# Attention and expert layer on one core: terms of Q and K interleaved by rows, one stacking DMA for both heads, the front work of batches 0 to 2 in another order

## Chip, cores and metric

One core of one Trainium2 chip runs the kernel. The metric is the device time of one execution, in microseconds (us), lower is better: the median of several runs.

## What is computed

The layer takes x [8, 256, 256] (8 batches of 256 tokens, 256 features) and a context of the same shape. It returns x + attention, and on top of that x + a mixture of experts:

```
q, k, v = LN(x) @ Wq.T, ctx @ Wk.T, ctx @ Wv.T      (16 heads of 16 features)
p       = softmax(where(masks, q @ k.T / 4, -inf))
x       = x + (p @ v) @ Wo.T + bo
gate    = softmax(LN(x) @ w_gate.T);  the best 2 of 8 experts for each token
x       = x + sum over the 2: score * (gelu(LN(x) @ W1[e] + b1[e]) @ W2[e] + b2[e])
```

Everything is float32. The masks are inputs (all true here).

## The kernel before, in words

**Two stages.** The attention stage works through 8 batches, in 64 steps of two heads (MP = 8 steps a batch). The expert stage then multiplies lists of 256 tokens with the weights of one expert at a time. Each engine has its own program over the same step numbers s = -16 to 84 (START, LAST), and semaphores tie them together. What is done at which step stands in tables: FRONT (lines 95 and 96) gives, for each batch n, the step 8n + offset of each piece of front work, and BACK, ROUTE and the LATE tables give what comes later. `due[s]` (lines 115 to 123) is what every engine reads, and the order of the work inside one step is the order of the `if` lines of that engine.

**Front work of a batch.** `load` (SP, lines 272 to 280) fetches x, ctxT and the mask of the batch. DVE takes the statistics of LN (`statistics`, line 454), POOL the inverse deviation (line 377) and the normalised rows (line 383; for batch 0 DVE does it, line 472). PE projects K from ctxT (`project`, line 747), turns the normalised rows (`turn_rows`, line 739), projects Q, and later V (`token_product`, line 755). These products are plain float32.

**Terms and stacking.** The scores need float32 precision from a faster type (fp32r), so a number is held as hi + lo. ACT writes hi (`split_high`, line 644), DVE the rest lo (`split_low`, line 447), both 128 partitions x 512 numbers in `flat`. `stack` (SP, lines 282 to 296) then copies them into K[n % 4] and Q[n % 4]. In these tiles head pair m of a batch is a slice of 256 numbers, the first head of the pair lives in partitions 0 to 63, the second in 64 to 127 (r = 0, 1; HALF = 64). Each half holds three terms of 16 rows, one after the other (TERMS = 3, D = 16): hi, hi, lo for K and hi, lo, hi for Q, so that one matmul over 48 rows gives three partial products. For each of the 3 terms and each half there is one DMA: 6 for K and 6 for Q, each of 128 KB, from 128 source partitions into 16 neighbouring ones:

```
for r in range(2):
    a = r * HALF + c * D
    done.after(sp.dma_start(dst[a:a + D]..., src[:, r, :]...))
```

**Two passes of scores.** In step s, `scores_for_max` (line 771) multiplies Q by K over the 48 rows into S1, and DVE takes the negated row maxima (`take_max`, line 479). LAG = 10 steps later `scores` (line 793) multiplies K by Q over 50 rows into S2: rows 48 and 49 of each half hold ones in K and the maxima as hi and lo in Q, so that the maxima are subtracted by the matmul. The maxima of a batch are turned by PE (`turn_maxima`), written to mT by ACT and put into Q by two DMAs that ACT issues (`maxima_out`, line 654). The ones are put into the four K tiles once, by 8 DMAs (`ones_rows`, line 298, at step -5). ACT then takes the exponential of S2 (line 678) and `weighted` (line 815) multiplies by V. S1 and S2 are one buffer each: S1 of step s waits for the maximum of step s - 1, S2 for the exponential before it.

**The masks' branch.** DVE reduces all masks to one flag (`least_mask`, line 432, called behind the first `q_split`), PE checks it by a matmul at step FLAG = -1 (`open_keys`, line 735), DVE writes any_mask (line 441), and PE reads it into a register and takes the branch without masks (lines 922 to 926). All steps s >= 0 of PE lie inside that branch.

**Small loads.** ACT issues all eight loads of weights and small inputs before anything else (`act_loads`, line 260). Many consumers wait for all small ones together (LOADS_SMALL).

**Where the zero rows come from.** `pool_constants` (line 340) makes ident, the zero tile and other constants on POOL. DVE starts its loop once all of them are there.

## Time and profile before

| what | us |
|---|---|
| median of 3 runs (583.44 to 587.05) | 586.22 |
| the profiled execution itself | 579.65 |
| its span, first to last instruction | 578.4 |

The profile comes from one execution. Its span is what the rows below add up to, and its own time is 1.25 us longer. PE is TensorE's matmuls, PEld its weight loads, DVE VectorE, ACT ScalarE, POOL GpSimd, SP the engine that issues most DMAs (SPq and ACTq are the queues' issue instructions). The attention stage fills the span up to about 266 us, the experts the rest. L789 is line 789 of the kernel. A mean of granted clock of 1.00 is 2.4 GHz, 0.50 is 1.2 GHz.

### The profile page before, as it was taken

To read this page: it belongs to the slowest core of one execution; us is meant where nothing else is said; L and a number is where in the kernel's file an instruction comes from. 1 tells how busy PE (TensorE), PEld (TensorE's weight loads), DVE (VectorE), ACT (ScalarE), POOL (GpSimd) and SP (SyncE) were. 2 spreads that over 40 slices of the span, in tenths; PEclk is the share of its full clock that TensorE was granted. 3 is DMA by queue.
4 is the path that set the end of the run, shared out by engine and by line. 5 is a ranking of instruction groups with operands and counts; after the bars stand their busy time and mean duration, and the time that the engine had idled before them with its cause. 6 is when DMAs were issued, how large, how long until landed. Compare 5 with 4: busy or idle time off the path is not lost.

```text
span 578.4 us, 10606 instructions
## 1 busy us (share of the span) xinstructions
PE 482.1 (83%) x3874; PEld 418.6 (72%) x3874; DVE 376.1 (65%) x736; ACT 344.8 (60%) x567; POOL 175.9 (30%) x191
## 2 busy tenths in 40 slices
PE   5546989999989858272299999699999999999994
PEld 4334656666756536151299999699999999999994
DVE  3455566866776744125568878568888788878871
ACT  1112566666566343211488788478887888778870
POOL 4320330352322654503302234204222432234324
PEclk9779799999999876656599999989999999999998
DMA  7976786867640911201555678969886878768713
GB/s 195 152 123 108 125 151 126 132 142 165 118 75 14 341 64 67 93 0 57 163 198 179 206 229 248 219 230 266 242 253 197 248 227 259 225 213 248 216 20 37
DMA packets 77637, 94.99 MB, mean 164 GB/s; under 512 B 7808, under 2 KB 70528, under 8 KB 77568
## 3 DMA queue, kind: packets, MB, share of 16 engines
q1 hardware_dynamic: 67344, 82.44, 52.4%
q0 software_dynamic: 8160, 10.38, 9.4%
q10 hardware_dynamic: 2080, 1.49, 0.9%
q8 instruction: 32, 0.52, 0.4%
q14 instruction: 21, 0.17, 0.1%
HBM read 63.96 MB, written 17.34 MB: 141 GB/s over the span
## 4 chain that ended last, share of the span: by engine, by line
PE 67%; issue 9%; DMA 7%; DVE 5%; ACT 4%; POOL 3%; SPq 2%; ACTq 1%; another core or an unknown queue 0%; POOLq 0%; DVEq 0%
PE h_bank L1079 21%; PE y_bank L1092 20%; PE bank L751 6%; PE bank L759 5%; PE bank L823 4%; PE S L789 3%; PE S L811 2%; PE bank L743 2%; PE x_bank L1063 2%; DMA cin<-in_ctxT 2%; DVE nmax L485 2%; POOL lists L404 2%; DMA xin<-in_x 2%; PE bank L831 1%; DMA xg<-lists 1%
## 5 line engine op out<-in xcount | busy, mean ns | idle before, releaser
L1186 POOL DMA_INDIRECT out<-y,slot x46 | 83.6, 1817 | 212.2 <-DVE y L1307 202.4
L1079 PE MATMUL h_bank<-xgT,W1p 128*128 128x256 f32 x1104 | 144.1, 288 | 1.8 <-DVE xgT L1278 1.8
L1079 PEld LDWEIGHTS h_bank<-xgT,W1p 128*128 128x128 f32 x1104 | 138.0, 194 | 2.2 <-issue 2.2
L1092 PE MATMUL y_bank<-W2p,hp 128*128 128x256 f32 x1104 | 136.0, 282 | 0.0
L1092 PEld LDWEIGHTS y_bank<-W2p,hp 128*128 128x128 f32 x1104 | 133.9, 188 | 0.0
L485 DVE TENSOR_REDUCE nmax<-S 128x4 f32<-128x1024 f32 x64 | 78.3, 1224 | 55.9 <-PE S L789 50.9
L683 ACT ACTIVATE prob<-S 128x1024 f32<-128x1024 f32 x64 | 65.8, 1028 | 43.2 <-PE S L811 26.7
L1293 DVE TENSOR_TENSOR hp<-hf,hp 128x512 fp32r<-128x512 f32 x92 | 63.6, 691 | 35.4 <-ACT hp L1152 35.3
L1253 DVE TENSOR_TENSOR W1p<-w_in,W1p 128x1024 fp32r<-128x1024 f32 x46 | 56.2, 1226 | 21.1 <-ACT W1p L1117 21.0
L1144 ACT ACTIVATE hf<-h_bank,b1c 128x256 f32<-128x256 f32 x120 | 49.7, 466 | 27.5 <-PE h_bank L1079 27.5
L1260 DVE TENSOR_TENSOR W2p<-w_in,W2p 128x1024 fp32r<-128x1024 f32 x46 | 56.3, 1225 | 10.1 <-ACT W2p L1126 10.1
L1152 ACT ACTIVATE hp<-hf 128x512 fp32r<-128x512 f32 x92 | 58.3, 634 | 2.9
L381 POOL TENSOR_TENSOR rstd<-ve,half 128x2 f32<-128x2 f32 x16 | 11.4, 714 | 155.7 <-DVE ve L470 155.6
L1117 ACT ACTIVATE W1p<-w_in 128x1024 fp32r<-128x1024 f32 x46 | 47.9, 1046 | 13.8 <-DMA w_in<-in_W 9.0
L1126 ACT ACTIVATE W2p<-w_in 128x1024 fp32r<-128x1024 f32 x46 | 48.0, 1046 | 0.0
L789 PE MATMUL S<-K,Q 48*128 48x256 f32 x256 | 33.4, 340 | 15.3 <-DVE nmax L485 13.1
L789 PEld LDWEIGHTS S<-K,Q 48*128 48x128 f32 x256 | 19.9, 192 | 34.0 <-DVE nmax L485 18.8
L404 POOL DMA_INDIRECT lists<-x2n,rows x32 | 32.7, 1022 | 26.5 <-DVE rows L587 18.1
L823 PE MATMUL bank<-prob,V 128*32 128x256 f32 x512 | 37.2, 412 | 1.2 <-ACT prob L683 1.2
L1144 ACT ACTIVATE hf<-h_bank,b1T 128x256 f32<-128x256 f32 x64 | 26.5, 466 | 16.5 <-PE h_bank L1079 16.5
L811 PE MATMUL S<-Q,K 50*128 50x256 f32 x256 | 29.5, 310 | 5.8 <-ACT prob L683 5.0
L751 PE MATMUL bank<-cin,WkT 128*128 128x256 f32 x64 | 22.6, 513 | 11.4 <-DMA cin<-in_ctxT 11.4
(140 smaller groups left out, 519.3 us busy)
## 6 DMA issues: line engine op xcount, KB each, us to landing
w_in<-in_W SPq DMA_DIRECT2D x46, 1024.0 KB, 8.9
K<-flat_k SPq DMA_DIRECT2D x48, 128.0 KB, 4.3
Q<-flat_q SPq DMA_DIRECT2D x48, 128.0 KB, 4.3
xg<-lists SPq DMA_DIRECT2D x23, 265.0 KB, 5.5
lists<-zero SPq DMA_DIRECT2D x17, 265.0 KB, 4.8
b_in<-in_b SPq DMA_DIRECT2D x23, 128.0 KB, 6.6
xin<-in_x SPq DMA_DIRECT2D x8, 256.0 KB, 4.9
cin<-in_ctxT SPq DMA_DIRECT2D x8, 256.0 KB, 5.3
```

The costliest lines, as they stand in the source:

```text
L485: max_done.after(dve.tensor_reduce(nmax[n % 4][:, :, :, m].rearrange("p t r -> p r t"), S1[:].rearrange("p r (t k) -> p r t k", t=TT), AX. ...
L683: exp_done.after(act.activation(prob[s % 4][:].rearrange("p r t l -> p (r t l)"), S2[:].rearrange("p r l -> p (r l)"), ACT.Exp, scale=SCALE))
L751: i = pe.matmul(b[:, m * L:(m + 1) * L], w[:, kc, m * P:(m + 1) * P], src[:, kc, :], start=(kc == 0), stop=(kc == KC - 1))
L789: i = pe.matmul(S1[:, r, t * L:(t + 1) * L], Q[n % HELD][a, m, t * P:(t + 1) * P], K[n % HELD][a, m, :], start=not masked, stop=(not maske ...
L823: i = pe.matmul(b[j * OS:(j + 1) * OS, 0:L], V[n % 3][:, t, r * MP + m, :], prob[(MP * n + m) % 4][:, r, t, :], start=(t == 0), stop=(t == ...
L1079: ins = pe.matmul(h_bank[pair][:, u, :], W1p[k][a][:, kc, m * P:(m + 1) * P], xgT[k][c][:, kc, :], start=(j == 0), stop=(j == len(terms) - 1))
L1092: ins = pe.matmul(y_bank[k][:, t, :], hp[k][a][:, m, t * P:(t + 1) * P], W2p[k][c][:, m, :], start=(j == 0), stop=(j == len(terms) - 1))
L1144: h_act.after(act.activation(hf[pair % 2][:, u], h_bank[pair][:, u], ACT.Gelu, bias=bias[:, m:m + 1]))
L1152: h_hi.after(act.activation(hp[i % 2][0][:, c], hf[pair % 2][:], ACT.Copy))
L1186: st_y[i % 4].after(pool.indirect_dma_start(out=out, out_offset=bass.IndirectOffsetOnAxis(ap=slot[i % 4][:, t:t + 1], axis=0), in_=y[i % 2 ...
L1260: w2_lo.after(dve.tensor_tensor(W2p[i % 2][1][:, c], w2_in[i % 2][:, c], W2p[i % 2][0][:, c].bitcast(F32), ALU.subtract))
L1293: h_lo.after(dve.tensor_tensor(hp[i % 2][1][:, c], hf[pair % 2][:], hp[i % 2][0][:, c].bitcast(F32), ALU.subtract))
```

## The change

**Layout.** The three terms of a row now lie in neighbouring partitions: term c of row d is partition 4d + c of a half (ROWS = 4), and the fourth partition of each group of four is spare. A half is 64 rows of 16 x 4. Both heads of a pair are written by the same DMA: 32 partitions, every fourth of 128, from the 128 source partitions. The weights' columns are reordered on the host to fit. The spare rows hold zeros in Q (but the four that receive the maxima, which one DMA of ACT writes) and in K zeros and two rows of ones in each half (`corner`); `spare_rows` fills them with two DMAs of 32 partitions x 8 KB a tile, at steps -12, 1, 3 and 5. For batches 4 to 7 one more small DMA clears the four rows of the maxima before Q is stacked. Both passes of scores now read all 64 rows.

**Order.** FIRST_FRONT gives batches 0, 1 and 2 steps of their own. PE does nothing for batch 1 before the branch; FLAG is -4. ACT's loads are spread over steps. ctxT is loaded ahead of x, and the masks ahead of the batch's own mask. Batch 1 is normalised by DVE. `unread` puts matmuls over 512 columns of bf16, whose result nothing reads, into PE's program: 12 at step -6, 12 at step 0, 3 at each of the steps 1 to 9.

```diff
     HELD = 4
+    ROWS = TERMS + 1
+    FIRST_MAX = ROWS * (D - 2) + TERMS
...
                  q=-7, q_split=-6, q_stack=-6, mask_q=-3, v=-1, v_out=0, mrep=7, mx=8)
+    FIRST_FRONT = {
+        0: dict(load=-16, ln1=-13, norm1=-11, residual=5, k=-11, k_split=-10, k_stack=-10, xn=-8, xT=-7, q=-7, q_split=-6,
+                q_stack=-6, mask_q=-3, v=4, v_out=5, mrep=7, mx=8),
+        1: dict(load=-5, ln1=0, norm1=1, residual=6, k=1, k_split=2, k_stack=2, xn=2, xT=3, q=3, q_split=4, q_stack=4,
+                mask_q=5, v=6, v_out=7, mrep=15, mx=16),
+        2: dict(load=5, ln1=7, norm1=8, residual=9, k=8, k_split=9, k_stack=9, xn=10, xT=11, q=11, q_split=12, q_stack=12,
+                mask_q=13, v=15, v_out=16, mrep=23, mx=24)}
...
         for name, o in FRONT.items():
-            due[MP * n + o][name] = n
+            due[FIRST_FRONT[n][name] if n in FIRST_FRONT else MP * n + o][name] = n
...
-        ones = sb(first, "ones", [2, MP * L])
+        line = sb(first, "line", [2 * D, L])
...
+        blank = zero[0:2 * D, 0:1, 0:L].to_broadcast([2 * D, MP, L])
+        corner = line[:].rearrange("p (o l) -> p o l", o=1).to_broadcast([2 * D, MP, L])
...
-        k_ones = signal("k_ones", 16)
+        k_ones = [signal(f"k_ones{i}", 16) for i in range(HELD)]
...
+        def act_loads(s):
+            if s == START:
+                ld_wk.after(act.dma_start(WkT[:], WkT_in.rearrange("(k p) f -> p k f", p=P)))
+                ld_wq.after(act.dma_start(WqT[:], WqT_in.rearrange("(k p) f -> p k f", p=P)))
+                ld_pad.after(act.dma_start(pad_c[:], pad_c_in))
+            if s == -4:
+                ld_wv.after(act.dma_start(WvT[:], WvT_in.rearrange("(k p) f -> p k f", p=P)))
+            if s == 1:
+                ld_bo.after(act.dma_start(bo_b[:], bo.rearrange("(o e) -> o e", o=1).to_broadcast([P, E])))
+            if s == 6:
+                ld_wo.after(act.dma_start(WoT[:], WoT_in.rearrange("(k p) f -> p k f", p=P)))
+            if s == 7:
+                ld_small.after(act.dma_start(WgT[:], wgT_in.rearrange("(k p) e -> p k e", p=P)))
+                ld_small.after(act.dma_start(b1T[:], b1T_in))
...
                     sp.wait_ge(mask_q.sem, TT * (n - 1))
+                ld_c[n % 2].after(sp.dma_start(cin[n % 2][:], c_d[n]))
                 ld_x[n % 2].after(sp.dma_start(xin[n % 2][:], x_d[n]))
-                ld_c[n % 2].after(sp.dma_start(cin[n % 2][:], c_d[n]))
+                if n == 0:
+                    ld_masks.after(sp.dma_start(masks_in[:], mask.rearrange("n q k -> (n q k)")
...
                 if n >= HELD:
                     sp.wait_ge(s2_done.sem, MP * (n - HELD + 1))
+                    if which == "q":
+                        done.after(sp.dma_start(over_heads(dst[FIRST_MAX:FIRST_MAX + 4 * ROWS:ROWS]), blank[0:4]))
                 sp.wait_ge(sem, end - 1)
                 for c, src in order:
                     if src is lo:
                         sp.wait_ge(sem, end)
-                    for r in range(2):
-                        a = r * HALF + c * D
-                        done.after(sp.dma_start(dst[a:a + D].rearrange("p m l -> p (m l)").bitcast(F32),
-                                                src[:, r, :].bitcast(F32)))
-
-            def ones_rows():
-                sp.wait_ge(dve_const.sem, 1)
-                for i in range(HELD):
-                    for r in range(2):
-                        a = r * HALF + TERMS * D
-                        k_ones.after(sp.dma_start(K[i][a:a + 2].rearrange("p m l -> p (m l)").bitcast(F32), ones[:]))
+                    done.after(sp.dma_start(dst[c:P:ROWS].rearrange("p m l -> p (m l)").bitcast(F32),
+                                            src[:].rearrange("p k l -> p (k l)").bitcast(F32)))
+
+            def over_heads(rows_):
+                return rows_.bitcast(F32)
+
+            def spare_rows(i):
+                if i == 0:
+                    sp.wait_ge(pool_rows.sem, 4)
+                q_stacked[i].after(sp.dma_start(over_heads(Q[i][TERMS:P:ROWS]), blank[:]))
+                k_ones[i].after(sp.dma_start(over_heads(K[i][TERMS:P:ROWS]), corner[:]))
 
...
                     load(now["load"])
-                    if now["load"] == 0:
-                        ld_masks.after(sp.dma_start(masks_in[:], mask.rearrange("n q k -> (n q k)")
-                                                    .rearrange("(p f) -> p f", p=P)))
                 if "k_stack" in now:
                     stack("k", now["k_stack"])
                 if "q_stack" in now:
                     stack("q", now["q_stack"])
-                if s == -5:
-                    ones_rows()
+                if s == -12:
+                    spare_rows(0)
+                if s in (1, 3, 5):
+                    spare_rows(s // 2 + 1)
...
         def pool_constants():
+            pool_rows.after(pool.memset(zero[:, :, 0:E], 0.0))
+            pool_rows.after(pool.memset(line[:], 1.0))
+            pool.wait_ge(pool_rows.sem, 2)
+            pool_rows.after(pool.affine_select(out=line[:], in_=line[:], compare_op=ALU.is_ge, fill=0.0,
+                                               base=2 - D, pattern=[[0, L]], channel_multiplier=1))
+            pool.wait_ge(pool_rows.sem, 3)
+            pool_rows.after(pool.affine_select(out=line[:], in_=line[:], compare_op=ALU.is_ge, fill=0.0,
+                                               base=D + 1, pattern=[[0, L]], channel_multiplier=-1))
...
-            pool_const.after(pool.memset(zero[:, :, 0:E], 0.0))
...
-                    if now["norm1"]:
+                    if now["norm1"] > 1:
...
                 if s == FLAG:
                     all_open()
+                if s == 1:
+                    dve.wait_ge(pe_misc.sem, filled_by("xn", 0))
+                    normalise(0, 1)
                 if "k_split" in now:
                     split_low("k", now["k_split"])
+                    if now["k_split"] == 0:
+                        least_mask()
                 if "q_split" in now:
                     split_low("q", now["q_split"])
-                    if now["q_split"] == 0:
-                        least_mask()
...
                 if n:
-                    act.wait_ge(*stacked(q_stacked if which == "q" else k_stacked, n - 1, 2 * TERMS))
+                    act.wait_ge(*(stacked(q_stacked, n - 1, ROWS) if which == "q" else stacked(k_stacked, n - 1, TERMS)))
...
             def maxima_out(n):
                 if n:
-                    act.wait_ge(*stacked(m_stacked, n - 1, 2))
+                    act.wait_ge(*stacked(m_stacked, n - 1, 1))
                 evacuate("mx", n, mT[:], lambda ps: ps[0:4 * MP, 0:L])
                 act.wait_ge(*emptied_at("mx", n))
                 if n >= HELD:
                     act.wait_ge(s2_done.sem, MP * (n - HELD + 1))
-                for r in range(2):
-                    a = r * HALF + TERMS * D
-                    m_stacked[n % HELD].after(act.dma_start(
-                        Q[n % HELD][a:a + 2].rearrange("p m l -> p (m l)").bitcast(F32),
-                        mT[2 * MP * r:2 * MP * (r + 1), :]))
+                m_stacked[n % HELD].after(act.dma_start(
+                    Q[n % HELD][FIRST_MAX:FIRST_MAX + 4 * ROWS:ROWS].rearrange("p m l -> p (m l)").bitcast(F32), mT[:]))
 
             def query_mask(n):
...
                 now = due[s]
+                act_loads(s)
...
                 if m == 0:
-                    pe.wait_ge(*stacked(k_stacked, n, 2 * TERMS))
-                    pe.wait_ge(*stacked(q_stacked, n, 2 * TERMS))
+                    pe.wait_ge(*stacked(k_stacked, n, TERMS))
+                    pe.wait_ge(*stacked(q_stacked, n, ROWS))
+                    if n < HELD:
+                        pe.wait_ge(k_ones[n].sem, 16)
...
-                        a = slice(r * HALF, r * HALF + TERMS * D)
+                        a = slice(r * HALF, (r + 1) * HALF)
                         i = pe.matmul(S1[:, r, t * L:(t + 1) * L], Q[n % HELD][a, m, t * P:(t + 1) * P], K[n % HELD][a, m, :],
...
                 if m == 0:
-                    pe.wait_ge(*stacked(m_stacked, n, 2))
+                    pe.wait_ge(*stacked(m_stacked, n, 1))
                 if s == 0:
-                    pe.wait_ge(k_ones.sem, 16 * 2 * HELD)
+                    for ones in k_ones:
+                        pe.wait_ge(ones.sem, 16)
...
-                        a = slice(r * HALF, r * HALF + TERMS * D + 2)
+                        a = slice(r * HALF, (r + 1) * HALF)
                         i = pe.matmul(S2[:, r, t * L:(t + 1) * L], K[n % HELD][a, m, t * P:(t + 1) * P], Q[n % HELD][a, m, :],
...
+            def unread(passes):
+                wide = onesb[:].rearrange("p (o f) -> p o f", o=1).to_broadcast([P, 512 // P, P])
+                for _ in range(passes):
+                    pe.matmul(S2[:, 0], onesb[:], wide, start=True, stop=True)
+
             for s in steps:
                 now = due[s]
+                if s < LAG:
+                    unread(UNREAD.get(s, 3 if s > 0 else 0))
...
-        FLAG = -1
-        LOADS_SMALL = act_loads()
+        FLAG = -4
+        UNREAD = {-6: 12, 0: 12}
...
-    heads_first = [w.T.reshape(-1, 2, 8, 16).transpose(0, 1, 3, 2).reshape(w.shape) for w in (L0_xattn_Wq, L0_xattn_Wk)]
+    heads_first = [w.T.reshape(-1, 2, 4, 2, 16).transpose(0, 3, 1, 4, 2).reshape(w.shape) for w in (L0_xattn_Wq, L0_xattn_Wk)]
```

## Rows read from the trace of the kernel before

**Rows 1.** The page, its slices of 14.46 us: busy tenths and granted clock

```profile
PE   5546989999989858272299999699999999999994
...
PEclk9779799999999876656599999989999999999998
DMA  7976786867640911201555678969886878768713
```

**Rows 2.** Stretches of 1 us: busy of PE, PEld, DVE, ACT, POOL; PEclk; DMA share; GB/s

```profile
4.00:5.00 1.00, 0.00 (x0) 0.00 (x0) 0.00 (x0) 0.04 (x1) 0.93 (x3) 1.00 1.10 387
...
15.00:16.00 1.00, 0.00 (x0) 0.00 (x0) 0.35 (x1) 0.60 (x1) 0.00 (x0) 1.00 1.12 128
...
24.00:25.00 1.00, 1.00 (x4) 0.77 (x3) 0.02 (x1) 0.60 (x1) 1.00 (x2) 0.50 1.00 113
25.00:26.00 1.00, 1.00 (x6) 0.90 (x5) 0.67 (x1) 0.00 (x0) 0.26 (x1) 1.00 0.06 17
...
58.00:59.00 1.00, 0.63 (x6) 0.43 (x8) 1.00 (x2) 0.51 (x1) 0.00 (x0) 1.00 0.91 196
59.00:60.00 1.00, 0.80 (x8) 0.55 (x7) 0.93 (x6) 0.52 (x1) 0.01 (x1) 0.56 1.15 133
...
66.00:67.00 1.00, 1.00 (x11) 0.67 (x9) 0.00 (x0) 0.31 (x1) 0.00 (x0) 1.00 0.00 0
```

**Rows 3.** The chain of waits, 0 to 75 us: start, length, what

```profile
14.92 5.51 DMA cin<-in_ctxT
...
26.65 1.26 issue
...
29.00 9.15 DMA xin<-in_x
...
51.43 4.86 DMA Q<-mT
```

**Rows 4.** The page, DMA issues

```profile
K<-flat_k SPq DMA_DIRECT2D x48, 128.0 KB, 4.3
Q<-flat_q SPq DMA_DIRECT2D x48, 128.0 KB, 4.3
...
lists<-zero SPq DMA_DIRECT2D x17, 265.0 KB, 4.8
```

**Rows 5.** The timeline, 0 to 75 us: start, length, instruction, idle before it

```profile
10.35 3.90 SPq L295 DMA_DIRECT2D K<-flat_k  x6
...
11.32 3.66 PE L751 MATMUL bank<-xT,WqT 128*128 128x256 f32 x8 [0.78 <-ACT xT L639]
...
15.99 3.77 SPq L295 DMA_DIRECT2D Q<-flat_q  x6
...
27.91 0.51 PE L789 MATMUL S<-K,Q 48*128 48x256 f32 x4 [1.50 <-issue]
...
28.45 1.23 DVE L485 TENSOR_REDUCE nmax<-S 128x4 f32<-128x1024 f32 x1 [1.68 <-PE S L789]
...
47.48 1.99 PE L759 MATMUL bank<-WvT,cin 128*128 128x256 f32 x8
...
55.16 0.50 PE L789 MATMUL S<-K,Q 48*128 48x256 f32 x4
...
58.82 0.55 PE L789 MATMUL S<-K,Q 48*128 48x256 f32 x4 [0.37 <-DVE nmax L485]
```

**Rows 6.** The timeline, from 75 us

```profile
77.37 0.50 PE L789 MATMUL S<-K,Q 48*128 48x256 f32 x4
```

**Rows 7.** The chain of waits, whole span, in the experts

```profile
298.84 2.85 PE h_bank L1079 x24
```

**Rows 8.** Groups by form on PE, 100 to 160 us

```profile
L789 PE MATMUL S<-K,Q 48*128 48x256 f32 x90 | 11.4, 329 | 0.0
L811 PE MATMUL S<-Q,K 50*128 50x256 f32 x88 | 9.0, 282 | 0.5 <-ACT prob L683 0.5
```

**Rows 9.** A stretch of 20 us in the middle of the attention, columns of group 2

```profile
120.00:140.00 20.00, 18.99 (x167) 13.12 (x158) 14.67 (x29) 13.11 (x20) 7.52 (x8) 1.00 0.80 150
```

More of the change, by code:

```diff
@@ L258, in kept @@
             return x2n[:, k:k + nb].rearrange("p b t w -> p (b t) w")
-        def act_loads():
-            ld_wk.after(act.dma_start(WkT[:], WkT_in.rearrange("(k p) f -> p k f", p=P)))
-            ld_wq.after(act.dma_start(WqT[:], WqT_in.rearrange("(k p) f -> p k f", p=P)))
-            ld_small.after(act.dma_start(pad_c[:], pad_c_in))
-            ld_wv.after(act.dma_start(WvT[:], WvT_in.rearrange("(k p) f -> p k f", p=P)))
-            ld_small.after(act.dma_start(bo_b[:], bo.rearrange("(o e) -> o e", o=1).to_broadcast([P, E])))
-            ld_wo.after(act.dma_start(WoT[:], WoT_in.rearrange("(k p) f -> p k f", p=P)))
-            ld_small.after(act.dma_start(WgT[:], wgT_in.rearrange("(k p) e -> p k e", p=P)))
-            ld_small.after(act.dma_start(b1T[:], b1T_in))
-            return ld_small.value
+        def act_loads(s):
[12 more added lines that the diff above has]
+                ld_small.after(act.dma_start(b1T[:], b1T_in))
         def sp_attention():
@@ L372, in residual @@
                 if n == 0:
-                    pool.wait_ge(ld_small.sem, LOADS_SMALL)
+                    pool.wait_ge(ld_bo.sem, 16)
                 for t in range(TT):
@@ L587, in list_rows @@
                 rows_done.after(dve.tensor_copy(rows[i % 2][:, 1, 0:nt], ends[:, 1, 0:nt]))
-            dve_const.after(dve.memset(ones[:], 1.0))
             dve.wait_ge(pool_const.sem, POOL_CONSTS)
@@ L902, in pe_attention @@
                     if now["logits"] == 0:
-                        pe.wait_ge(ld_small.sem, LOADS_SMALL)
+                        pe.wait_ge(ld_small.sem, 16 * 2)
                     logits(now["logits"])
```

7 lines of the change are left out of this document (4 added, 3 removed).

## Prediction

> **What bounds the kernel now.** I read the page's slices first, then the chain of waits and the timeline of the first 75 us, and the same rows later for comparison. The slices show three regimes [rows 1]. In slices 1 to 4 (0 to 58 us) PE is busy 4 to 6 tenths while DMA is at 6 to 9, and the clock is often below full. From about 66 us PE is full: 18.99 of 20 us at 1.00 in the stretch [rows 9]. After 266 us the experts fill PE again. So the middle cannot gain from faster transfers: nothing there waits for one for long. What can move is the first 60 us, and what it gains should carry through, since all that follows is tied to it by order and not by time.
>
> In the front, four waits are to be seen [rows 3]. PE waits for batch 1's ctxT (5.51 us, landing at 20.4) although it has nothing to do with step 0; it stands ahead of the branch. The branch costs 1.26 us. DVE waits 9.15 us for batch 2's x, and step 10 waits 4.86 us for the maxima's DMA. The landmarks are the scores' first matmuls: step 0 at 27.91, step 10 at 55.16, step 12 at 58.82 [rows 5], step 18 at 77.37 [rows 6].
>
> Why transfers are slow here: at 15 us, with stacking alone in flight, the engines are saturated (share 1.12) at 128 GB/s; at 4 us, with the loads alone, they are as busy at 387 [rows 2]. A stacking DMA writes 16 partitions, a load 128. The K and the Q of batch 0 are 2 x 768 KB, 12 us at that rate, so Q lands about 24 to 25 us.
>
> **The change part by part.** Times are of the profiled execution.
>
> *The stacking.* Per batch 12 DMAs of 128 KB become 6 of 256 KB. SP's issue is 3.77 us for 6 [rows 5], so 1.9 for 3. The bytes stay. The rate is the unknown: below, it stays at 128 GB/s; above, it reaches the 387 of the loads [rows 2]. I take 250, because a DMA here still only writes 32 partitions and both its ends are in the same memory. Then Q of batch 0 (issued from 15.7 us on, like now) needs 3 us, and the last part lands by its median 4.3 us [rows 4] behind its issue at 17: at 21.3. It lies beside PE's work below (step 0 comes at 22.5), with 1.2 us to spare. In the steady part it takes load off the DMA engines, and gives nothing.
>
> Here the Trainium skill has a rule (SBUF — State Buffer, section "Door 1: The DMA port swizzle"): a range of 16 neighbouring partitions reaches 4 of the 16 DMA ports and measured 104 GB/s there, and every fourth of 128 would reach all of them. By it the rate would rise, as taken; with a rate that stays, the sum is that of the third rival.
>
> *Spare rows.* Eight DMAs of 256 KB (2 MB) replace eight of 16 KB; SP's issue stays eight instructions. At 250 GB/s they are 8 us of the DMA engines, at 128 they are 16. The first pair is issued near 3 us behind the loads, while 0.8 MB of weights and biases leaves that place for later; I take the two as even. The others stand at steps 1, 3 and 5: each puts 1.2 us of issue and 2 us of transfer ahead of K, Q or nothing of batch 1, which step 8 needs some 10 us later. Cost nothing; if that cover were gone, 2 us.
>
> *The start.* ctxT first: 0.5 us earlier. Four more short instructions of POOL hold DVE back by up to 1 us. I call both ends even: q's projection ends at 15.0 as now (11.32 + 3.66 [rows 5]). Bounds -0.5 to +1.
>
> *Ahead of step 0.* k and v of batches 1 and 0 leave. What stays: 12 unread passes, the flag, the branch, 12 passes more. The trace has no bf16 pass of 512 columns. The nearest rows are the experts' one-pass matmuls of 256 columns, 2.85 us for 24 [rows 7], so 0.119 each, and 0.24 for 512 at full clock, 0.48 at half. Twelve are 2.9 us (5.7 at half). The flag's matmul and DVE's answer are 0.5 by estimate, the branch 1.26: 1.7. So step 0 is at 15.0 + 2.9 + 1.7 + 2.9 = 22.5, against 27.91: 5.4 earlier. With both bursts at half clock it would be 28.1, nothing gained. The flag itself is ready in time: the reduction of the masks now comes behind K's split (about 11 us) and not behind Q's.
>
> Another price for a pass stands in the Trainium skill (TensorE: Matmul & The Clock Gate, "Back-to-back issue gap"): 216 ns warm for 512 columns. By it the two bursts would be 0.6 us shorter; no row here shows it.
>
> *Steps 0 to 9.* Without front work a step is 0.51 of S1 and 1.23 of DVE's maximum, 1.83 with the gaps (steps 10 and 11 are 3.66, from 55.16 to 58.82 [rows 5]); three passes (0.72) run while DVE works, so they are free in such a step. A step that also holds a projection (1.99 at full clock [rows 5]) is 0.5 + 1.99 + 0.72 = 3.2. Five are such (k and q of batch 1, v of 0 and 1, k of 2): 16.0. Five are bare: 9.2. The maxima of batch 0 at step 8 put DVE's and PE's small work between: 0.9 as estimate. Sum 26.1, against 55.16 - 27.91 = 27.25 now: 1.1 earlier, 6.5 at step 10. DVE takes over one normalisation from POOL and has room behind PE in steps 1 to 3. Batch 2's x and ctxT are issued at step 5, about 35 us, on queues that are then nearly empty, and land by 41, before steps 7 and 8: the wait of 9.15 us goes. Of the waits that are added, PE's on the ones of its own tile, SP's on POOL's first rows (K's stacking is queued behind it) and POOL's on bo alone (batch 2's load waits for that residual) are all met some us ahead. ACT's loads of bias and weights cost it 0.5 us each in steps where it has little to do.
>
> *Steps 10 to 18.* The normalised rows and q of batch 2 move here from steps 8 and 9. Step 11 becomes 3.0 (its two scores 1.0 + 1.99) and not 1.83: 1.2 later. The maxima's DMA is one instead of two and goes out with quiet queues, so S2 of step 0 no longer waits. Against that stands the clock. It is 0.56 at 59 us, behind a stretch in which PE was busy 0.63, and full again only at 66 [rows 2]. In these 6.5 us PE works without a pause at half speed, so about 3 us go. In the new order PE has q's projection and the turning of rows just there, 2.6 us more work in steps 10 and 11, and 27 + 24 passes before. I take it that the clock holds: 3 earlier. Bounds 0 and 3.5.
>
> *Steady part.* Both score passes go from 48 and 50 rows to 64. The groups of 48 and 50 rows are 329 and 282 ns [rows 8]: more rows are not slower; both already share the array in two halves. I take nothing; the bound by the difference to the 128-row expert matmul (0.119 against 0.11 a pass) is +0.01 x 512, 5 us, and it would have to show as longer groups. SP and ACT issue less there; PE does not wait for them. One small DMA more for batches 4 to 7: nothing.
>
> *Sum.* 5.4 + 1.1 - 1.2 + 3 = 8.3 earlier at step 18, carried to the end: 579.65 - 8.3 = 571.35 in the profiled execution. The runs' median stands 6.57 above that execution; I take the same distance for both kernels: 586.22 - 8.3 = 577.9.
>
> **The rivals.**
>
> *The clock falls again in or around steps 0 to 18* (the gain of 3 fails, or one burst runs at half speed, 2.8). For it: in the trace it fell at 59 us while DVE and ACT set the pace of PE [rows 2]. Against it: the passes fill just these gaps. Gain 5.3: 580.9.
>
> *The spread rows do not move faster.* For it: the only row with stacking alone is 128 GB/s [rows 2], and nothing in the trace says whether the 16 partitions or something else sets that. Then Q of batch 0 lands 3 us later, at 24.3, step 0 gains 3.6, and the rest holds: gain 6.5, 579.7.
>
> *More comes out.* The passes are shorter than taken and the front has fewer gaps; also DVE's and ACT's waits of the steady part shrink with the empty queues. Another 4: 573.9.
>
> *Slower: the unread passes at half clock.* PE becomes the bound of steps 0 to 9. At half clock a pass is 0.48, a projection 3.66 (q's at 11 us [rows 5]), S1 and the turning of rows by estimate 0.8 and 1.1: 8 + 18.3 + 1.1 + 27 x 0.48 = 40.4 for the ten steps, and step 0 at 28.1; step 10 at 68.5, 13.3 late. From full to half clock the whole costs 14.3 + 5.6 = 19.9, so the gain of 8.3 is used up when the clock is at half for more than 42% of this stretch. At 60%: 11.9 lost, 8.3 regained, 3.6 slower: 589.8. For it: the slices' clock is 7 tenths from 14 to 43 us [rows 1], and it is 0.50 still at 24 us [rows 2]. Against it: it rose at 25 us after PE had been busy since ctxT's landing at 20.4 [rows 2, 3], and here PE is busy from about 5 us on with short breaks.
>
> **How the numbers follow.** Forecast 0.50 (577.9; its own range 574.5 to 580.5), clock falls 0.18 (580.9), no faster transfer 0.10 (579.7), more 0.12 (573.9), slower 0.10 (589.8). One per cent, what can be told from no change here, is 5.9 us, so 580.4 is the border. Faster: 0.46 of the forecast, 0.12 of more, 0.06 of the transfer's and 0.03 of the clock's: 0.67. Slower 0.08 of the last; the same gets 0.25. The range leaves out the last rival and a little at the low end: 571.5 to 584.0.
>
> **What would show it.** In the profile of the changed kernel: step 0's S1 at 22 to 23 us and step 10's near 48.5; the stacking at 200 GB/s and more with queues empty between; the granted clock 1.00 from 15 us to 180; the stretch 120 to 140 as full as now; everything from 70 us on some 8 us earlier; groups of 64 rows at the same ns. The forecast would be wrong with: rows of `unread` of 0.4 us each, S1 waiting on Q's DMA at step 0 or 8, or a stretch of 20 us in the middle in which PE is busy less than its present 18.99 us.

## The result: 14.9 us faster, more than the 8.3 forecast and just outside the range

The changed kernel takes 570.62 us (median of 4 runs, 565.6 to 571.1); the kernel before, on the same chip, 585.52 (583.44 to 587.05). The ratio is 0.9729, 95% interval 0.9665 to 0.9792. Forecast were 577.9 and a range of 571.5 to 584.0.

Sessions and chips differ: the kernel before had a median of 578.42, 582.66, 583.79 and 585.52 us in the four sessions of this study. So totals are compared as ratios within one session. The two profiled executions (579.65 before, 570.19 after) are only 9.5 apart. That of before was a quick one, 5.9 below the median here and below all four runs; that of after is 0.4 below its median.

The page of the changed kernel, its slices (14.2 us each), answering to [rows 1]:

```profile
PE   5888899999988576441699999599999999999994
...
PEclk9998999999988767555599999799999999999998
DMA  6683533444108321103627879868878778677713
```

PE is at 8 tenths from the second slice on, where it was at 4 to 6, and DMA, at 6 to 9 tenths before, has one slice at 8 and is at 3 to 6 in the others from the first to the seventh. The same from the issues on the page [rows 4]:

```profile
K<-flat_k SPq DMA_DIRECT2D x24, 256.0 KB, 2.4
...
lists<-zero SPq DMA_DIRECT2D x17, 265.0 KB, 3.8
```

Twice the bytes per DMA land in 2.4 us instead of 4.3. Stretches of 1 us with K's and Q's stacking under way, one around the clock's fall, and the stretch in the middle (columns of [rows 2]; answers to [rows 2, 9]):

```profile
11.00:12.00 1.00, 1.00 (x6) 0.87 (x6) 1.00 (x1) 0.00 (x0) 0.00 (x0) 1.00 1.05 404
...
16.00:17.00 1.00, 0.00 (x0) 0.00 (x0) 0.00 (x0) 0.00 (x0) 0.00 (x0) 1.00 1.04 402
...
48.00:49.00 1.00, 1.00 (x4) 0.73 (x4) 1.00 (x3) 0.68 (x1) 0.00 (x0) 0.50 0.03 8
...
120.00:140.00 20.00, 19.36 (x184) 13.70 (x181) 13.84 (x26) 12.60 (x19) 7.67 (x8) 1.00 0.39 134
```

The DMA engines are as saturated as before (1.05 and 1.04 against 1.12) and move three times as much: 402 GB/s against 128. In the middle their share is halved, 0.39 against 0.80, and PE is busier, 19.36 us against 18.99. That last number is the first sign of what the forecast missed.

The timeline of the front, answering to [rows 5, 6]:

```profile
9.29 1.87 SPq L314 DMA_DIRECT2D K<-flat_k  x3
...
10.80 1.97 PE L778 MATMUL bank<-xT,WqT 128*128 128x256 f32 x8 [0.78 <-ACT xT L668]
...
12.61 2.75 PE L891 MATMUL S<-onesb 128*128 128x512 bf16 x12
...
17.05 2.76 PE L891 MATMUL S<-onesb 128*128 128x512 bf16 x12 [1.69 <-issue]
...
19.74 0.50 PE L818 MATMUL S<-K,Q 64*128 64x256 f32 x4
...
44.65 0.50 PE L818 MATMUL S<-K,Q 64*128 64x256 f32 x4 [1.32 <-DVE nmax L512]
...
50.67 0.51 PE L818 MATMUL S<-K,Q 64*128 64x256 f32 x4
...
65.29 0.50 PE L818 MATMUL S<-K,Q 64*128 64x256 f32 x4
```

Step 0 starts at 19.74 (27.91 before), step 10 at 44.65 (55.16), step 12 at 50.67 (58.82), step 18 at 65.29 (77.37). Of the four long waits of [rows 3] three are gone; the branch's is left (1.48 us, before 1.26), as forecast. The chain of waits of the changed kernel, 5 to 62 us, goes through PE and DVE almost alone and names no DMA. Four of its pieces, with the branch between the two bursts of passes:

```profile
12.77 2.59 PE S L891 x12
15.57 1.48 issue
17.05 2.76 PE S L891 x12
...
23.99 0.65 PE S L891 x3
```

### The profile page after: what moved, and what is told of

Same layout as the page of the kernel before. It is cut to its first block, busy times and chain, and to the rows that moved or that the text cites. A ratio compares the mean times of both kernels' runs of the same rounds, so it can differ in the third digit from the quotient of the medians.

```text
span 569.0 us, 10658 instructions
## 1 busy us (share of the span) xinstructions
PE 487.9 (86%) x3925; PEld 419.8 (74%) x3925; DVE 375.3 (66%) x737; ACT 344.8 (61%) x567; POOL 174.1 (31%) x192
## 4 chain that ended last, share of the span: by engine, by line
PE 69%; issue 9%; DVE 7%; POOL 4%; ACT 4%; DMA 3%; SPq 2%; ACTq 1%; another core or an unknown queue 0%; POOLq 0%; DVEq 0%
PE h_bank L1116 21%; PE y_bank L1129 20%; PE bank L778 5%; PE bank L786 5%; PE S L818 4%; PE bank L853 3%; DVE nmax L512 3%; PE S L841 2%; PE bank L770 2%; PE x_bank L1100 2%; POOL lists L431 2%; PE S L891 2%; DMA xg<-lists 1%; PE bank L861 1%; PE bank L870 1%
## 5 line engine op out<-in xcount | busy, mean ns | idle before, releaser
L818 PEld LDWEIGHTS S<-K,Q 64*128 64x128 f32 x256 | 19.6, 189 | 26.4 <-issue 14.0
L818 PE MATMUL S<-K,Q 64*128 64x256 f32 x256 | 33.0, 337 | 6.3 <-DVE nmax L512 5.6
L841 PE MATMUL S<-Q,K 64*128 64x256 f32 x256 | 29.1, 308 | 2.5 <-ACT prob L709 1.2
L1100 PE MATMUL x_bank<-ident,xg 128*128 128x128 f32 x92 | 14.9, 287 | 18.0 <-DMA xg<-lists 18.0
```

The lines of the kernel that those rows point to most:

```text
L818: i = pe.matmul(S1[:, r, t * L:(t + 1) * L], Q[n % HELD][a, m, t * P:(t + 1) * P], K[n % HELD][a, m, :], start=not masked, stop=(not maske ...
```

## The experiments

Three sessions of four kernels, the first on one chip, the other two on another. In each the kernel before ran beside them; kernels of one session are compared with each other. The edits below are shortened to what matters. "Step 18" is the start of the first matmul of the scores for the maxima in that step, in the profiled execution.

### The layout alone, the order alone, both without passes

**The kernel before, again.** No edit.

> The kernel before once more, unchanged, for a second profile. The first profile's execution (579.65 us) lies 5.9 us below the median of the timed runs (585.5). If the clock's dips in the front and the tail differ from execution to execution, this profile shows other stretches below 1.00 and a span near 584; if the first profile is typical, the span is 578 to 580 and the offset lies outside of the span.

Measured: 579.42 us, ratio 1.0014 [0.9987, 1.0041]. Step 0 at 28.25, step 10 at 57.12, step 18 at 78.66, step 50 at 164.62. Its profiled execution took 580.51, 1.1 above its own median: the distance between profile and median that the prediction started from belongs to the one execution and not to the kernel. The next three kernels are compared with this one.

**The layout alone.** The changed kernel with its new rows and stacking, but the old order of loads and front work, the flag at step -1, and no unread passes.

```diff
-            due[FIRST_FRONT[n][name] if n in FIRST_FRONT else MP * n + o][name] = n
+            due[MP * n + o][name] = n
-                    unread(UNREAD.get(s, 3 if s > 0 else 0))
+                    unread(0)
-        FLAG = -4
+        FLAG = -1
```

> The new layout and its DMAs alone (rows interleaved, 3 DMAs a stack, one DMA for the maxima, spare rows), with the order, the flag step and the loads of before and no unread passes. Theory A (ACT's second maxima DMA lay on PE's path once in each batch, 0.65 us each): the steady batches are 0.65 us shorter than before, 7 times, 4.5 us, and the front gains 1 to 3 us from Q landing earlier: 577 to 580. Theory B (the whole gain is the front's order): 584 to 586.

Measured: 561.15 us, ratio 0.9704 [0.9669, 0.9740]. Step 18 at 68.29: 10.4 earlier than the base. This is the whole gain of the change, without the reordering. The two profiled executions are 17.4 apart, as the medians are (17.3), and the steps tell where it comes from: 10.4 up to step 18, 4.2 from there to step 62 (118.40 us instead of 122.56), 2.5 from step 62 to the experts' first matmul, 0.4 behind it.

**The order alone.** The new order, flag, loads and passes, with the old rows: six stacking DMAs of 16 neighbouring partitions and two for the maxima.

```diff
-                    done.after(sp.dma_start(dst[c:P:ROWS].rearrange("p m l -> p (m l)").bitcast(F32),
-                                            src[:].rearrange("p k l -> p (k l)").bitcast(F32)))
+                    for r in range(2):
+                        a = r * HALF + c * D
+                        done.after(sp.dma_start(dst[a:a + D].rearrange("p m l -> p (m l)").bitcast(F32),
+                                                src[:, r, :].bitcast(F32)))
```

> The new order alone: FIRST_FRONT, flag at step -4, loads spread, unread passes; the old layout with 6 DMAs a stack, two for the maxima, 48 and 50 rows. Theory A: step 0 waits for Q's last DMA at about 23 to 24 us and not 19.7, steady batches stay as before, so 4 us of start and the ten steps are gained: 578 to 581. Theory B: 570 to 573, as the changed kernel.

Measured: 576.46 us, ratio 0.9982 [0.9948, 1.0016]: not to be told from no change. Its chain of waits, 5 to 62 us, shows why:

```profile
17.92 6.59 DMA Q<-flat_q
...
40.86 5.68 DMA Q<-flat_q
```

The order brings the work forward, and then PE waits for slow stacking, at step 0 and again at step 8. Step 0 comes at 24.65, step 18 at 73.90, 4.8 before the base; steps 18 to 50 then take 87.31 instead of 85.96. The median of ten runs is 2.0 below that of the kernel before, which is within the noise.

**Both, without the 51 unread passes.** Nothing that is computed differs.

```diff
-                    unread(UNREAD.get(s, 3 if s > 0 else 0))
+                    unread(0)
```

> The changed kernel without any of the 51 unread passes. If the passes hold the clock: step 0 comes earlier by some us (two bursts of 2.75 us go) but projections of the front run at half clock (3.7 for 2.0 us), and step 18 is 2 to 5 us later than in the changed kernel: 572 to 576. If the passes are only work of PE: 566 to 569, faster than the changed kernel.

Measured: 560.44 us, ratio 0.9700 [0.9667, 0.9733]. Step 18 at 65.25, the same as with the passes (65.29), and 3.0 earlier than with the layout alone; of that 0.7 us is left in the median, less than can be told. The granted clock over two stretches, without passes:

```profile
20.00:45.00 25.00, 19.01 (x86) 13.36 (x86) 15.93 (x26) 4.77 (x9) 6.54 (x8) 0.93 0.74 211
45.00:70.00 25.00, 21.28 (x198) 14.75 (x199) 18.33 (x28) 16.63 (x25) 6.05 (x8) 1.00 0.53 191
```

and in the base:

```profile
20.00:45.00 25.00, 18.49 (x61) 13.39 (x61) 10.09 (x17) 3.37 (x6) 9.04 (x10) 0.57 0.77 116
45.00:70.00 25.00, 19.41 (x126) 12.80 (x125) 13.97 (x19) 10.09 (x15) 4.53 (x5) 0.77 0.62 111
```

The 0.93 is too high. The trace's first record of the clock in this execution says full and stands at 26.83 us, and the view prints 1.00 ahead of a first record. The matmuls tell otherwise: ahead of it a projection of batch 1 takes 3.58 us, behind it the next takes 1.99.

```profile
20.75 0.79 PE L818 MATMUL S<-K,Q 64*128 64x256 f32 x4 [5.74 <-DMA Q<-flat_q]
...
23.59 3.58 PE L778 MATMUL bank<-cin,WkT 128*128 128x256 f32 x8
...
29.36 1.99 PE L778 MATMUL bank<-xT,WqT 128*128 128x256 f32 x8
```

With half clock up to 26.83 the stretch comes to about 0.80 (my estimate); the passes hold it at 1.00 in the changed kernel. So the passes do hold the clock, and it gains nothing by step 18. The first line shows one thing more: without passes PE sits idle 5.74 us ahead of step 0 until Q's stacking has landed, and most of the passes stand in this wait.

### What makes the transfers fast, and what the maxima's DMA is worth

**The changed kernel, again.** No edit.

> The changed kernel once more, unchanged, on the chip of the other experiments. Front order and passes worth something: it beats the layout alone (561.2 on the other call) by 2 us or more, 557 to 559. Worth nothing at the end: 561 to 563. Its first profile lost some 8 us between 185 and 224 us against the kernel without passes; if that is chance, this profile reaches the experts near 266 us, if it comes with the change, near 274.

Measured: 566.96 us, ratio 0.9705 [0.9652, 0.9758]. Step 0 came at 23.07 here, for one reason:

```profile
11.25 3.75 PE L778 MATMUL bank<-xT,WqT 128*128 128x256 f32 x8 [0.78 <-ACT xT L668]
14.80 3.79 PE L891 MATMUL S<-onesb 128*128 128x512 bf16 x12
```

In the execution shown above the same matmuls took 1.97 and 2.75 us. By these lengths the clock was still at half (1.2 GHz) in q's projection and part of the first burst here, and full (2.4 GHz) there. The trace's first record of the clock, which says full, fits: it stands at 16.88 us here and at 9.05 there (the view by stretches prints 1.00 ahead of it in both). Step 12 is 1.7 later than there, at 52.41. The experts' first matmul is at 274.95, where the expectation asked whether 266 or 274: the same as in the first profile.

**The maxima by two DMAs.** The new layout, but the four rows of the maxima go out two by two, as before.

```diff
-                m_stacked[n % HELD].after(act.dma_start(
-                    Q[n % HELD][FIRST_MAX:FIRST_MAX + 4 * ROWS:ROWS].rearrange("p m l -> p (m l)").bitcast(F32), mT[:]))
+                for r in range(2):
+                    a = FIRST_MAX + 2 * ROWS * r
+                    m_stacked[n % HELD].after(act.dma_start(
+                        Q[n % HELD][a:a + 2 * ROWS:ROWS].rearrange("p m l -> p (m l)").bitcast(F32),
+                        mT[2 * MP * r:2 * MP * (r + 1), :]))
```

> The changed kernel with the maxima put into Q by two DMAs of 2 rows each and not by one of 4. Theory A (the second issue of 0.6 us on ACT delays the exponential and then PE, once a batch): steady batches go from 20.32 back to 20.97 us, step 50 comes 4 to 4.6 us later than in the changed kernel, the whole 4 to 5 us slower. Rival (the batches are shorter because the stacking frees the DMA queues): step 50 within 0.5 us, no difference.

Measured: 569.60 us, ratio 0.9762 [0.9706, 0.9818], 2.6 slower than the changed kernel beside it, less than the 4 to 5 expected, and the intervals overlap. The trace decides: a batch of eight steps (26 to 34) takes 20.96 us, as in the kernel before (97.72 to 118.69: 20.97), and not 20.32 as in the changed kernel (84.88 to 105.20).

**Each stacking DMA in two.** Each writes 16 partitions, every fourth of 64; twelve DMAs of 128 KB a batch, as before. Its source is 64 partitions with both heads (before: 128 partitions with one head).

```diff
-                    done.after(sp.dma_start(dst[c:P:ROWS].rearrange("p m l -> p (m l)").bitcast(F32),
-                                            src[:].rearrange("p k l -> p (k l)").bitcast(F32)))
+                    for r in range(2):
+                        a = r * HALF
+                        done.after(sp.dma_start(dst[a + c:a + HALF:ROWS].rearrange("p m l -> p (m l)").bitcast(F32),
+                                                src[a:a + HALF].rearrange("p k l -> p (k l)").bitcast(F32)))
```

> The changed kernel, rows interleaved as there, but each stacking DMA in two of 16 partitions (every fourth of 64), 6 a stack of 128 KB as before the change. If the spread of the partitions is what made the transfers fast, they stay at 250 GB/s or more and land in about 2.5 us, and the time is within 1 us of the changed kernel but for SP's longer issue (3.8 for 1.9 us a stack). If the size or number of the DMAs is what counts, the rate falls back to about 130 GB/s and the landing to over 4 us, step 8 or 16 waits, and the kernel is 3 us or more slower.

Measured: 566.27 us, ratio 0.9711 [0.9656, 0.9766]: equal to the changed kernel. From the page's DMA issues of this kernel:

```profile
K<-flat_k SPq DMA_DIRECT2D x48, 128.0 KB, 2.3
```

and of the order alone, with the same number and size of DMAs into 16 neighbouring partitions:

```profile
K<-flat_k SPq DMA_DIRECT2D x48, 128.0 KB, 4.3
```

So it is the spread over partitions that makes the transfers fast, not the size or number of the DMAs. SP's issue (3.79 us for six) came back and cost nothing: step 18 is at 67.03, in the changed kernel beside it at 67.04.

One thing did change together with the spread, here and in the changed kernel: a piece copied in one go is 512 numbers long (2,048 bytes) and not 256. No run has the old length with the new spread in the stacking. The spare rows are the nearest to it. They are written in pieces of 1,024 bytes, from SBUF, into every fourth partition, and from 8 to 9 us of the changed kernel they alone are in flight:

```profile
8.00:9.00 1.00, 0.63 (x2) 0.00 (x0) 0.48 (x2) 0.33 (x1) 0.48 (x1) 1.00 0.66 232
```

232 GB/s at a share of 0.66 would be 350 at a full one, against 114 (128 at 1.12) with neighbouring partitions; both are my estimates from these rows. In the trace's records a packet of 1,024 bytes takes 46 ns there and 148 ns in the old stacking (medians), one of 2,048 bytes in the new stacking 84 ns. So short pieces are fast too where they are spread. The source of the spare rows is 32 partitions and not 128, so this is strong evidence, not a clean test.

**Filler passes in the last third.** The kernel without front passes, with unread passes in PE's waits of the last 57 us ahead of the experts (137 by the page; the 132 of the expectation is a miscount). Nothing that is computed differs.

```diff
+            def fill(name, n):
+                wide = onesb[:].rearrange("p (o f) -> p o f", o=1).to_broadcast([P, 512 // P, P])
+                for _ in range(FILL.get((name, n), 0)):
+                    pe.matmul(S1[:, 0], onesb[:], wide, start=True, stop=True)
```

> The kernel without passes in the front, but with 132 unread passes in PE's idle stretches of the end of the attention (into S1, free from step 65 on): ahead of y of batches 6 and 7, the last counts, logits and ao, and 48 ahead of the experts' first tile. If the half clock there costs time on the path: matmuls of 220 to 275 us at full clock, 5 to 10 us less than without passes: 551 to 556. If the chain there is DVE's, POOL's and the DMAs' and PE's speed is hidden: 559 to 562, or slower where a pass stands in the way.

Measured: 562.58 us, ratio 0.9625 [0.9556, 0.9694], 4.4 less than the changed kernel beside it; the intervals overlap by a little, but all its runs (557.4 to 563.3) lie below all of that kernel's (565.1 to 571.4). Expected were 551 to 556 from totals on the other chip, and 5 to 10 us less than without passes. The experts' first matmul starts at 267.96 instead of 274.95, and the clock from 225 to 250 us is at 1.00 instead of 0.57.

### The passes on one chip, and whose time an issue is

**The kernel without passes, again.**

> The changed kernel without any of its 51 unread passes, again, now beside the changed kernel on the same chip. Theory (the layout makes the gain, the passes nothing): within 0.4% of the changed kernel, ratio to the kernel before 0.970 to 0.975; step 18 at 65 to 67 us. Rival (the passes hold the clock and so carry part of the gain): 3 us or more slower than the changed kernel, ratio 0.978 or above, with the clock at 0.5 somewhere between step 0 and step 10.

**The changed kernel beside it.**

> The changed kernel again, beside the kernel without its passes on the same chip. Theory: ratio to the kernel before 0.970 to 0.975, no more than 0.4% from the kernel without passes. Rival (the passes carry part of the gain): at least 3 us faster than the kernel without them.

Measured: 568.75 us without passes, ratio 0.9758 [0.9670, 0.9846]; 568.99 with them, ratio 0.9758 [0.9692, 0.9823]. The passes give nothing that can be measured, though step 18 was 2.0 later with them (66.70 against 64.66): in the front they cost. With q's projection slow (3.37 and 3.75 us), step 0 comes at 20.05 without them and at 22.73 with them; with the projection at 1.97, at 18.47 (the kernel with fillers) and at 19.74. Both ratios are 0.001 above what was expected.

**The kernel before, with one of its two maxima DMAs issued by SP.**

```diff
-                for r in range(2):
-                    a = r * HALF + TERMS * D
-                    m_stacked[n % HELD].after(act.dma_start(
-                        Q[n % HELD][a:a + 2].rearrange("p m l -> p (m l)").bitcast(F32),
-                        mT[2 * MP * r:2 * MP * (r + 1), :]))
+                a = TERMS * D
+                m_stacked[n % HELD].after(act.dma_start(
+                    Q[n % HELD][a:a + 2].rearrange("p m l -> p (m l)").bitcast(F32), mT[0:2 * MP, :]))
+            def other_maxima(n):
+                sp.wait_ge(*emptied_at("mx", n))
+                if n >= HELD:
+                    sp.wait_ge(s2_done.sem, MP * (n - HELD + 1))
+                a = HALF + TERMS * D
+                m_stacked[n % HELD].after(sp.dma_start(
+                    Q[n % HELD][a:a + 2].rearrange("p m l -> p (m l)").bitcast(F32), mT[2 * MP:4 * MP, :]))
```

> The kernel before with one of its two maxima DMAs issued by SyncE instead of ScalarE; nothing else differs. Theory (ScalarE's second issue of 0.65 us a batch delays the exponential and by it the tensor engine): steps 18 to 50 take 83.4 us instead of 86.0, each batch 20.3 instead of 21.0, and the whole is 2.5 to 5 us shorter, ratio 0.992 to 0.996. Rival 1 (it is the landing of the maxima through few ports that costs, not the issue): batches stay at 21.0 and the ratio at 1.000. Rival 2 (SyncE's added wait holds its queue, and loads and stacks behind it come late): ratio above 1.002.

Measured: a batch takes 20.33 us (96.02 to 116.35), steps 18 to 50 take 83.37 instead of 86.06. That is the changed kernel's batch (20.32) from one issue moved to SP, so the issue was the cause. The layout of the rows plays no part in it, for here it is the old one. The whole gained less than expected: 581.25 us, ratio 0.9973 [0.9936, 1.0009], which does not exclude 1. In its profile the experts start at 286.47, so in this execution what was won by step 50 was lost again in the last third, where the clock is low (0.50 to 0.65 in five of the six stretches of 5 us from 195 to 225 us).

The timelines at the same place, batch 3's maxima. The kernel before, two issues by ACT:

```profile
93.25 1.30 ACTq L663 DMA_DIRECT2D Q<-mT  x2
...
94.65 1.02 ACT L683 ACTIVATE prob<-S 128x1024 f32<-128x1024 f32 x1 [1.43 <-PE bank L823]
...
95.73 0.51 PE L811 MATMUL S<-Q,K 50*128 50x256 f32 x4 [0.29 <-ACT prob L683]
...
96.98 1.35 PE L751 MATMUL bank<-xT,WqT 128*128 128x256 f32 x5 [0.75 <-ACT xT L639]
```

The kernel before with one by SP:

```profile
91.01 0.66 SPq L303 DMA_DIRECT2D Q<-mT  x1
91.01 0.65 ACTq L672 DMA_DIRECT2D Q<-mT  x1
91.77 1.03 ACT L691 ACTIVATE prob<-S 128x1024 f32<-128x1024 f32 x1 [0.78 <-PE S L819]
```

ACT's exponential stands behind its own issue: it is idle 1.43 us in the one and 0.78 in the other. The row puts the 1.43 down to a matmul of `bank`, but the row of ACTq above fills it. Behind the exponential come the copies out of PSUM, xT last, and PE waits 0.75 us for that.

**The best version.** No front passes, the fillers of the last third, and the maxima's one DMA issued by SP, none by ACT (the edit is the one above, with the new rows).

> The changed kernel without unread passes at the front, with 132 filler passes in the last third, and with the maxima DMA issued by SyncE, so that ScalarE issues none for the maxima. Theory (an issue on ScalarE costs its 0.65 us a batch): steps 18 to 50 take 80.8 us against 83.4 in the changed kernel, batches 19.7 instead of 20.3; the whole 3 to 7 us shorter than the changed kernel on this chip (the fillers' part of it 2 to 4), ratio 0.955 to 0.965. Rival (one issue was already hidden, and only the second of the kernel before was not): steps 18 to 50 stay at 83.4, and the ratio is that of the fillers alone, 0.962 to 0.970.

Measured: 558.32 us, ratio 0.9603 [0.9524, 0.9682], 10.7 less than the changed kernel beside it (568.99). It is the fastest here. A batch takes 19.90 (81.13 to 101.03), 0.42 less than with one issue by ACT, of 0.66 expected: PE waits 0.22 for xT where it waited 0.67 to 0.75.

```profile
76.55 0.68 SPq L321 DMA_DIRECT2D Q<-mT  x1
76.77 1.02 ACT L713 ACTIVATE prob<-S 128x1024 f32<-128x1024 f32 x1 [0.24 <-PE S L845]
...
79.21 1.99 PE L782 MATMUL bank<-xT,WqT 128*128 128x256 f32 x8 [0.22 <-ACT xT L677]
```

Steps 18 to 50 take 83.29 all the same, because the clock fell to half at 136 us and a projection took 3.64 instead of 1.99; expected were 80.8. How the 10.7 us divide between SP's issue and the fillers was not run alone on this base.

## Why the prediction was wrong in size

The direction was right. The size failed in three places: the steady part was costed at nothing and gave 2.7 us by step 50, the front's terms were 3.8 us too small, and the distance from profile to median was carried over to a kernel that did not have it.

**Right.** The direction; the place of the front's gain; that transfers are what the front waits for; that 64-row score groups are no slower (330 and 276 ns from 100 to 160 us, against 329 and 282 [rows 8]); the branch and flag (1.69 us, taken as 1.7); twelve passes 2.75 us, taken as 2.9. A pass is 0.22 us. By the Trainium skill (TensorE: Matmul & The Clock Gate, "Back-to-back issue gap") the gap of an isolated matmul over 512 columns is 216 ns at full clock; the trace agrees, with 0.65 us for three. The 131 ns that the same section of the Trainium skill gives for a sustained stream are not seen here: twelve in a row take 2.59 us of the chain.

```profile
L818 PE MATMUL S<-K,Q 64*128 64x256 f32 x92 | 11.6, 330 | 1.6 <-DVE nmax L512 1.6
L841 PE MATMUL S<-Q,K 64*128 64x256 f32 x92 | 9.1, 276 | 0.0
```

**The failed step: "SP and ACT issue less there; PE does not wait for them".** The steady part was costed at nothing. Steps 18 to 50 take 83.35 instead of 86.06: 0.64 to 0.77 in each of the four batches. PE at 18.99 of 20 us was read as full, and the 1.0 us that was left was not looked at; the two waits of 0.29 and 0.75 us a batch, behind ACT, make that up, and ACT's issue stands in the same queue as its exponential. In the changed kernel, with one issue, the second of them is 0.67:

```profile
82.96 1.99 PE L778 MATMUL bank<-xT,WqT 128*128 128x256 f32 x8 [0.67 <-ACT xT L668]
```

(Of the 0.65 a batch, 0.37 is to be seen as less idle time of PE, 18.99 to 19.36; the rest was not followed.) The maxima by two DMAs and the kernel before with one moved to SP show it from both sides. One of the rivals named ACT's waits, but put them down to empty queues; it was the issue.

**The mis-sized terms of the front.** Step 18 was forecast 8.3 earlier (69.1); it came at 65.29, and at 67.04 and 66.70 when run again: 10.3 to 12.1.

- *Step 0, forecast 22.5.* It came at 19.74 where q's projection was fast, and at 23.07 where it was not. The forecast had the projection at 3.66; measured were 1.97 and 3.75. The order does not decide this: with the same kernel both were seen. Of the 2.8 us by which 19.74 beats the forecast, 2.2 lie ahead of the projection's end (12.77 instead of 15.0); that it was the fast case which was profiled is luck.
- *Ten steps, forecast 26.1.* 24.91 and 24.92 in the two executions, 1.2 less.
- *Steps 10 to 18, forecast 20.4.* 20.64 and 19.05. The clock did fall, at 47 us, but for 3 us and not 6.5. The clock rival was partly right, with a fall that cost 1.2 us (q's projection in 3.19).
- *The rate, taken as 250 GB/s.* 402 to 412 were measured, above the upper bound of 387. The rule that the prediction weighed, of the Trainium skill (SBUF — State Buffer, "Door 1: The DMA port swizzle"), says that 16 neighbouring partitions reach few ports. The rates agree with it (128 GB/s with neighbours, 402 to 412 with the spread), though no trace here shows the ports. The split DMAs show the other side of it: 16 partitions that are spread are fast too, 128 KB in 2.3 us. Their total is 207 GB/s from 11 to 12 us, which is 128 KB in each 0.63 us of SP's issue.

**Credit given to the wrong part.** The forecast put 6.5 of its 8.3 on the new order, and feared slow transfers as a rival that would still leave 6.5. With the old rows and the new order almost nothing was left (0.9982), and with the new rows alone everything was there (0.9704). On top of the new rows the order brought step 18 3.0 earlier and the median 0.7. For step 0 that rival was right: 3.6 us earlier (28.25 to 24.65), as it said. It missed that the same transfers set the pace again at batch 1: the chain goes through Q's DMA for 6.59 us ahead of step 0 and for 5.68 ahead of step 8. The passes, credited with 3 us of held clock, held it and gave nothing.

**The sum, and the step from the profile to the median.** In the profiled pair step 50 is 14.8 us earlier (163.43 and 148.64): 12.1 from the front and 2.7 from the steady part. "Carried to the end" did not hold there: 5.3 us were lost again (0.8 up to step 62, 4.0 from there to the experts' first matmul, 0.5 behind it). So the forecast of the profiled execution, 571.35, is only 1.2 from the 570.19 measured, and that is luck: 6.5 too little up to step 50 stands against 5.3 lost behind it. What took the median out of the range is the last term. "I take the same distance for both kernels" was 6.57 us, and for the changed kernel it measured 0.4. Of the 7.3 us between forecast and median 6.1 are this term. It rested on one quick execution; in later profiles the distance was 1.1 us the other way (the kernel before) and 4.5 and 1.8 the other way (the changed kernel). That the medians differ by 14.9, nearly what the steps show up to step 50, stays untraced: the one execution of the kernel before that was profiled beside them was not a typical one.

**Open.** From step 62 to the experts' first matmul the kernels take 81 to 89 us, and it goes by session more than by kernel. It is 81.2 to 83.6 in the four kernels of the first session, the kernel before among them, and 86.5 to 89.0 in the second and third without fillers, with passes in the front (88.4 to 89.0 in the changed kernel) or without (88.9), and with the old rows too (88.6, one maxima DMA by SP). In the profiled pair it is 84.8 and 88.8 (the experts' first matmul stands at 284.05 and 274.10; the 266 us of the prediction are too early). Part is the clock: with the fillers it is 83.0 and 82.1, and they are worth about 4 us. Part is a wait of DVE before its maximum of step 63, which the trace gives to nothing in this core:

```profile
192.42 1.23 DVE L512 TENSOR_REDUCE nmax<-S 128x4 f32<-128x1024 f32 x1 [2.46 <-remote]
```

It is 1.9 to 3.3 us long in 9 of the 14 profiles, the kernel before among them, and absent in five, four of them the kernels of the first session. Its cause was not tried, nor that of the difference between the sessions.

## What to carry to other kernels

Before an order is rewritten, look at which transfers are slow while the DMA engines are saturated: here a strided choice of partitions tripled the rate and gave all that the reordering was meant to give. A DMA issue costs 0.65 us of the engine that makes it; here, on an engine with work in the critical loop, it was paid in full the second time and by two thirds the first, and moving it to SP won that back. A stretch in which PE is 95% busy still has 5% to win, so read its last waits before writing "nothing". And do not carry the distance between one profiled execution and a median over to another kernel: profile twice first.

## What was not expected of the hardware

- 404 GB/s from 11 to 12 us, with K's stacking under way, whose both ends are in SBUF, and 412 from 26 to 27 with batch 1's; 128 with the same bytes before. The DMA engines' share is 1.05 and 1.06 in the one and 1.12 in the other.
- The same program finds the clock full at 11 us in one execution and, by the length of its matmuls, at half in the next (q's projection 1.97 and 3.75 us), and this moves step 0 by 3.3 us. By step 18 it is 1.8. The granted clock that the view prints ahead of the trace's first clock record is no reading: 1.00 stands beside matmuls of 634 ns each, which take 379 ns at full clock.
- The clock can fall in a full stretch: in the best version PE was busy 5.00 us of each of the stretches of 5 us from 120 to 140, and the granted clock was 1.00 until 136 us and then half, 0.66 over the last 5 us:

```profile
125.00:130.00 5.00, 5.00 (x48) 3.52 (x48) 3.85 (x9) 2.16 (x4) 3.28 (x4) 1.00 0.31 112
130.00:135.00 5.00, 5.00 (x49) 3.82 (x48) 3.90 (x9) 3.65 (x6) 1.25 (x2) 1.00 0.28 107
135.00:140.00 5.00, 5.00 (x23) 3.54 (x23) 1.89 (x5) 1.62 (x2) 0.00 (x0) 0.66 0.30 108
```
